# Causal mask of the row maxima moved from a matmul into VectorE's maximum, and query chunks made in every second step

## What is computed

```python
q = (x @ wq).reshape(b, s, H, QH).transpose(0, 2, 1, 3)      # b=2, s=1024, H=16, QH=192
q_pe = _rope(q_pe, cos, sin)
scores = jnp.einsum('bhqd,bhkd->bhqk', qs, ks_) * scale
causal = jnp.tril(jnp.ones((s, s), dtype=bool))
scores = jnp.where(causal, scores, jnp.finfo(scores.dtype).min)
attn = jax.nn.softmax(scores, axis=-1)
out = jnp.einsum('bhqk,bhkd->bhqd', attn, v)
```

## Time and profile before

| | |
|---|---|
| median of 3 runs | 1459.19 us (1459.08 to 1462.78) |
| profiled execution: its time, its span | 1459.05 us, 1457.2 us |
| PE busy (share of the span) | 1227.6 us (84%) |
| POOL busy | 961.9 us (66%) |
| DVE busy | 844.7 us (58%) |
| ACT busy | 626.2 us (43%) |
| mean granted clock of PE | 0.93 |

### The profile page before, as it was taken

How to read it: one execution, slowest core, us unless ns; L and a number is a source line. 1 busy time by engine, 2 the same in 40 slices (tenths; PEclk the granted TensorE clock), 3 DMA queues, 4 the chain that set the end, 5 groups by cost and what they waited for, 6 DMA issues and landing times. The chain is left out here.

```text
span 1457.2 us, 18876 instructions
## 1 busy us (share of the span) xinstructions
PE 1227.6 (84%) x5880; PEld 881.1 (60%) x5881; DVE 844.7 (58%) x1551; ACT 626.2 (43%) x1069; POOL 961.9 (66%) x700
## 2 busy tenths in 40 slices
PE   6974699999992489988998897689889998998797
PEld 5863455555551356666666666556666666666686
DVE  4578522222224667766676654767766776673567
ACT  3220233333320245565565564135655565565242
POOL 2025768888875457877788776557876787776454
PEclk9986799999995789999999998779999999999899
DMA  9348335555555000000000000000000000002001
GB/s 327 118 153 216 98 60 82 82 80 81 80 79 167 8 8 8 8 1 8 8 8 1 1 1 12 8 8 8 8 1 8 8 8 1 1 1 64 1 8 51
DMA packets 66509, 68.28 MB, mean 47 GB/s; under 512 B 15072, under 2 KB 59680, under 8 KB 66304
## 3 DMA queue, kind: packets, MB, share of 16 engines
q1 hardware_dynamic: 48336, 43.42, 10.0%
q0 software_dynamic: 15168, 20.72, 9.2%
q10 hardware_dynamic: 2928, 3.15, 0.7%
HBM read 46.17 MB, written 21.10 MB: 46 GB/s over the span
## 5 line engine op out<-in xcount | busy, mean ns | idle before, releaser
L1512 POOL TENSOR_TENSOR att_prob_lo<-att_prob,att_prob_hi 128x1024 fp32r<-128x1024 f32 (+1 forms) x160 | 346.7, 2167 | 114.1 <-ACT att_prob_hi L1448 114.0
L1555 DVE TENSOR_REDUCE att_peak<-all_bank 128x1 f32<-128x512 f32 (+3 forms) x384 | 207.4, 550 | 208.8 <-PE all_bank L1343 140.4
L1359 PE MATMUL all_bank<-att_q_hl,sequence_k_hl 128*128 128x512 f32 (+1 forms) x960 | 263.6, 385 | 0.0
L1382 PE MATMUL all_bank<-att_prob_hi,sequence_v_hl 128*128 128x512 f32 (+1 forms) x640 | 201.6, 396 | 35.3 <-POOL att_prob_lo L1512 19.1
L1441 ACT ACTIVATE att_prob<-all_bank 128x1024 f32<-128x1024 f32 (+1 forms) x160 | 150.6, 941 | 175.9 <-PE all_bank L1365 174.7
L1359 PEld LDWEIGHTS all_bank<-att_q_hl,sequence_k_hl 128*128 128x128 f32 x960 | 170.0, 192 | 26.1
L1340 PE MATMUL all_bank<-sequence_k_hl,att_q_hl 128*128 128x512 f32 (+3 forms) x384 | 171.0, 449 | 8.7 <-DVE att_peak L1555 8.3
L1448 ACT CAST att_prob_hi<-att_prob 128x1024 fp32r<-128x1024 f32 (+1 forms) x160 | 154.2, 964 | 5.1
L1327 PE MATMUL all_bank<-sequence_x_hl,sequence_w_hl 128*128 128x512 f32 x384 | 115.0, 438 | 46.3 <-DVE all_xT L1550 38.7
L1489 POOL TENSOR_TENSOR all_xT<-all_xT 128x512 f32<-128x512 f32 x64 | 82.4, 1288 | 106.1 <-DVE all_xT L1550 105.7
L916 PE MATMUL all_bank<-early_w_gu,moe_xgT 128*128 x316 | 148.9, 554 | 3.6 <-issue 2.4
(11 more groups left out here) (244 smaller groups left out, 2103.6 us busy)
## 6 DMA issues: line engine op xcount, KB each, us to landing
sequence_w_raw<-wqk_rows SPq DMA_DIRECT2D x16, 256.0 KB, 2.7
early_w_gu<-in_gate SPq DMA_DIRECT2D x16, 224.0 KB, 5.7
early_w_gu<-in_up SPq DMA_DIRECT2D x16, 224.0 KB, 5.8
early_w_down<-in_down SPq DMA_DIRECT2D x1, 3584.0 KB, 19.8
sums<-early_zero SPq DMA_DIRECT2D x18, 128.0 KB, 3.7
all_xT<-in_xT SPq DMA_DIRECT2D x4, 512.0 KB, 7.6
all_x_tok<-in_x SPq DMA_DIRECT2D x1, 2048.0 KB, 16.3
x_rows<-all_x_tok SPq DMA_DIRECT2D x4, 512.0 KB, 3.0
```

What stands on the lines that cost most here:

```text
L1359: nc.tensor.matmul(ps, k_hl[:, ks, j * P:(j + 1) * P], q_hl[n % 2][:, qs, :, i * BW + q0:(i + 1) * BW], start=g == 0, stop=False)
L1382: mm = nc.tensor.matmul(out, v_hl[:, vs, j, :], part[:, u % 3, half * WIDE:half * WIDE + 2 * w].rearrange("p (h m) -> p h m", h=2), start= ...
L1512: nc.gpsimd.tensor_tensor(prob_lo[:, u % 3, 0:w], prob[:, u % 2, 0:w], prob_hi[:, u % 3, 0:w].bitcast(F32), ALU.subtract).then_inc(lo_sb, 1)
L1555: nc.vector.tensor_reduce(peak[:, n % 2, part, t // 2, h, t % 2:t % 2 + 1], piece_ps[y % 2][:, 0:w], AX_X, ALU.max).then_inc(peak_sb, 1)
```

## The change

Two things change. In a diagonal piece the mask matmul is gone; DVE adds a table (`late_wide`, zeros and at its right end the causal triangle) to the piece and takes the maximum in the same instruction, writing the sum back to PSUM and the maximum to `peak`. For a row with two pieces the maximum of the first starts the second's, so that L1564 is gone. And the tables that place the work are new: query chunks in steps 0, 2, 4 and 6 instead of 0 to 3; eight of a pair's own pieces in its steps 0 to 3, the other 16 in steps 4 to 9 of the pair before (before: 3 own, 21 from step 2 of the pair before); weights, products and inversions moved to later steps.

```diff
-    NEXT_PIECES = [0, 0, 1, 2, 3, 3, 3, 3, 3, 3]
-    OWN_PIECES = [2, 1] + [0] * (NG - 2)
+    QUERY_AT = {0: 0, 2: 1, 4: 2, 6: 3}
+    NEXT_PIECES = [0, 0, 0, 0, 1, 3, 1, 3, 4, 4]
+    OWN_PIECES = [2, 3, 2, 1] + [0] * (NG - 4)
...
-    INVERT_AT = {1: (-1, 0), 2: (-1, 1), 3: (0, 0), 4: (0, 1), 5: (1, 0), 6: (1, 1), 7: (2, 0), 8: (2, 1)}
-    PRODUCT_AT = {3: -1, 5: 0, 7: 1, 9: 2}
+    INVERT_AT = {0: [(-1, 0)], 1: [(-1, 1)], 3: [(0, 0), (0, 1)], 5: [(1, 0)], 7: [(1, 1)], 8: [(2, 0)], 9: [(2, 1)]}
+    PRODUCT_AT = {0: -2, 2: -1, 4: 0, 8: 1}
...
                     mm = nc.tensor.matmul(ps[:, 0:w], q_hl[n % 2][:, 0, h, t * P:(t + 1) * P],
-                                          k_hl[:, 0, k0:k0 + w], start=True, stop=not diagonal)
-                    if diagonal:
-                        mm = nc.tensor.matmul(ps[:, w - P:w], bf["late_q"], bf["ident"], start=False, stop=True)
+                                          k_hl[:, 0, k0:k0 + w], start=True, stop=True)
...
-                    if x == 4 and n + 2 < PAIRS:
+                    if x == 7 and n + 2 < PAIRS:
                         weights_high(n + 2)
...
-                        if 1 <= x <= QC:
-                            q_low(n + 1, x - 1)
-                        if x < QC:
-                            rotate(n + 1, x)
+                        if x - 1 in QUERY_AT:
+                            q_low(n + 1, QUERY_AT[x - 1])
+                        if x in QUERY_AT:
+                            rotate(n + 1, QUERY_AT[x])
                     if u + AHEAD < STEPS:
                         low(u + AHEAD)
-                    if x == 5 and n + 2 < PAIRS:
+                    if x == 8 and n + 2 < PAIRS:
                         weights_low(n + 2)
...
                     dve.wait_ge(max_mm, n * NP + y + 1)
-                    nc.vector.tensor_reduce(peak[:, n % 2, part, t // 2, h, t % 2:t % 2 + 1], piece_ps[y % 2][:, 0:w],
-                                            AX_X, ALU.max).then_inc(peak_sb, 1)
+                    if diagonal:
+                        if part:
+                            dve.wait_ge(peak_sb, n * NP + y - 1)
+                        nc.vector.tensor_tensor_reduce(ps, ps, bf["late_wide"][:, WIDE - w:WIDE], 1.0, half if part else MASKED,
+                                                       ALU.add, ALU.max, whole).then_inc(peak_sb, 1)
+                    else:
+                        nc.vector.tensor_reduce(half, ps, AX_X, ALU.max).then_inc(peak_sb, 1)
...
-                    if i >= NB // 2:
-                        top = whole[:, n % 2, i]
-                        nc.vector.tensor_tensor(top, peak[:, n % 2, 0, i], peak[:, n % 2, 1, i], ALU.max).then_inc(whole_sb, 1)
-                        dve.wait_ge(whole_sb, n * (NB // 2) + i - NB // 2 + 1)
```

More of the change, by code:

```diff
@@ L63, in const_columns @@
     for name, width in (("ident", P), ("cos", QT * ROPE), ("sin", QT * ROPE), ("before", P), ("iota", P), ("headmask", P),
[L64 removed]
+                        ("late_q", P), ("late_k", P), ("late_cols", P), ("row", 1)):
         at[name] = (n, n + width)
@@ L96, in const_table @@
     put("late_k", np.where(f >= p, MASKED, 0.0))
-    q = np.arange(2 * P)[None, :] - P
-    put("late_cols", p == np.maximum(q + 1, 0))
+    put("late_cols", p == f + 1)
     put("row", p)
@@ L1253, in phase_attention @@
     block_needs = [1 + max(y for y in range(NP) if pieces[y][0] // 2 == i) for i in range(NB)]
-    NEXT_PIECES = [0, 0, 1, 2, 3, 3, 3, 3, 3, 3]
-    OWN_PIECES = [2, 1] + [0] * (NG - 2)
-    FIRST_PIECES = [3, 3, 2] + [0] * (NG - 3)
-    EARLY = NP - sum(FIRST_PIECES)
-    INVERT_AT = {1: (-1, 0), 2: (-1, 1), 3: (0, 0), 4: (0, 1), 5: (1, 0), 6: (1, 1), 7: (2, 0), 8: (2, 1)}
-    PRODUCT_AT = {3: -1, 5: 0, 7: 1, 9: 2}
+    QUERY_AT = {0: 0, 2: 1, 4: 2, 6: 3}
+    NEXT_PIECES = [0, 0, 0, 0, 1, 3, 1, 3, 4, 4]
+    OWN_PIECES = [2, 3, 2, 1] + [0] * (NG - 4)
+    EARLY = NP - sum(OWN_PIECES)
+    INVERT_AT = {0: [(-1, 0)], 1: [(-1, 1)], 3: [(0, 0), (0, 1)], 5: [(1, 0)], 7: [(1, 1)], 8: [(2, 0)], 9: [(2, 1)]}
+    PRODUCT_AT = {0: -2, 2: -1, 4: 0, 8: 1}
     def aside(n, x):
[L1264 to L1267, removed]
+        out = [("query", n + 1, QUERY_AT[x])] if n + 1 < PAIRS and x in QUERY_AT else []
+        out += [("piece", n, EARLY + sum(OWN_PIECES[:x]) + a) for a in range(OWN_PIECES[x])]
         if n + 1 < PAIRS:
@@ L1334, in piece @@
                     _, n, y = item
-                    t, h, _, k0, w, diagonal = pieces[y]
+                    t, h, _, k0, w, _ = pieces[y]
                     if n * NP + y >= 2:
@@ L1471, in _ @@
                     n, x, _, _ = at(u)
-                    made = n + 1 < PAIRS and x < QC
+                    made = n + 1 < PAIRS and x in QUERY_AT
                     if u + AHEAD < STEPS:
@@ L1476, in _ @@
                     if made:
-                        q_high(n + 1, x)
+                        q_high(n + 1, QUERY_AT[x])
                     if x in last_of:
                         sums(n, last_of.index(x))
-                    if x == 4 and n + 2 < PAIRS:
+                    if x == 7 and n + 2 < PAIRS:
                         weights_high(n + 2)
@@ L1536, in _ @@
                         product(n * NB + PRODUCT_AT[x])
+                product(PAIRS * NB - 2)
             @block.vector
@@ L1552, in peaks @@
                 def peaks(n, y):
-                    t, h, part, _, w, _ = pieces[y]
+                    t, h, part, _, w, diagonal = pieces[y]
+                    half, whole = (peak[:, n % 2, a, t // 2, h, t % 2:t % 2 + 1] for a in range(2))
+                    ps = piece_ps[y % 2][:, 0:w]
                     dve.wait_ge(max_mm, n * NP + y + 1)
-                    nc.vector.tensor_reduce(peak[:, n % 2, part, t // 2, h, t % 2:t % 2 + 1], piece_ps[y % 2][:, 0:w],
-                                            AX_X, ALU.max).then_inc(peak_sb, 1)
+                    if diagonal:
[5 more added lines that the diff above has]
+                        nc.vector.tensor_reduce(half, ps, AX_X, ALU.max).then_inc(peak_sb, 1)
                 def spread(n, i):
-                    top = peak[:, n % 2, 0, i]
+                    top = peak[:, n % 2, 1, i]
                     dve.wait_ge(peak_sb, n * NP + block_needs[i])
-                    if i >= NB // 2:
-                        top = whole[:, n % 2, i]
-                        nc.vector.tensor_tensor(top, peak[:, n % 2, 0, i], peak[:, n % 2, 1, i], ALU.max).then_inc(whole_sb, 1)
-                        dve.wait_ge(whole_sb, n * (NB // 2) + i - NB // 2 + 1)
                     if n:
@@ L1600, in _ @@
                         beside(item)
-                    if x in INVERT_AT:
-                        i, half = INVERT_AT[x]
+                    for i, half in INVERT_AT.get(x, ()):
                         if n * NB + i >= 0:
```

18 lines of the change are left out of this document (10 added, 8 removed).

## The result

The changed kernel took **1505.08 us** (median of 4 runs, 1503.77 to 1505.52) and the kernel before 1459.13 in the same rounds: ratio 1.0311, 95% interval 1.0289 to 1.0333. It is 3.1% slower; the forecast was 1523 in a range of 1462 to 1548. The profiled execution took 1505.52 us with a span of 1503.7.

The account below looks back on a forecast made before the run. PE was taken as the nearest bound, with query-to-sums chains behind two waits. Pairs at 47.85 us (+0.43, 14 times: 6.0) plus 1.6 for last pairs gave 1467; 56 of clock loss made 1523 us, range 1462 to 1548.

Parts of the forecast that it names:

- Pause A: PE's wait before V(1), the first value product of step 1: from 6.9 to 10.0 us after step 0 starts.
- Pause B: PE's wait before V(3), step 3's value product: work done at 18.4, product at 21.98, so 3.5 us.
- Step 0 to V(1): Stretch from a pair's start to step 1's first value product: same chain as before, 10.03 us.
- rival 3: Faster: the 1.26 us wait before V(3) is really POOL's, so a pair takes 44.2 us, 1414 in all; chance of faster 0.15.
- rival 1: The clock does not fall in the two pauses in steps 0 to 3: 1467 us; chance 0.10.
- the 0.53 us that V(6) was to wait: New PE wait after V(3), for block 2's sums: chain 8.5 us against 8.0 of PE work, 0.33 + 0.2.
- 25.34 and the wait: V(3) to the next step 0: 25.34 us of PE work, 24.92 before, plus 0.53 waiting for block 2's sums.
- I take 2.0 each: Clock loss behind each of the two pauses, between 1.5 and 2.7 us: 4.0 a pair, 56 us over 14 pairs.
- the forecast 0.8 for the eighth: Last pair of each sequence: five pieces more and two masks less, +0.8 us each, 1.6 in all.
- the 0.88 that was named as a sign: Sign in the changed trace: granted clock in a mid-phase pair below 1.00, about 0.88.
- The maxima were to cost 3.2 us more: DVE per pair: 16 second instructions at 0.2 us add 3.2, two dropped maxima of halves save 1.3.
- The accumulator's instruction: Second, 128x1 DVE instruction of each masked maximum: taken as 0.2 us, bounds 0.17 and 0.67.

Follow-up runs that it names:

- Experiment 3: Changed kernel with ACT's four copies of the sums placed ahead of its q_hl copy; 1421.83 us, ratio 0.9752.
- the filled kernel: Changed kernel with 6 and 12 useless 512-column matmuls a pair added on PE in steps 1 and 3; 1465.37 us, ratio 1.005.
- experiment 12: Kernel before with mask on DVE, ACT's copies of the sums first, and DVE doing the rope before the step's first maximum; 1375.43 us, ratio 0.9442.
- experiment 5: Changed kernel with query chunks back in steps 0 to 3, all else as changed; 1443.33 us, ratio 0.9905.
- experiment 6: Kernel before with ACT's four copies of the sums ahead of its q_hl copy; 1455.14 us (7 runs, 1436 to 1457).
- experiment 7: Kernel before with the mask on DVE and ACT's copies of the sums ahead of its q_hl copy; 1430.45 us.
- 8: Changed kernel with query chunks back in steps 0 to 3 and ACT's copies of the sums ahead of its q_hl copy; 1429.48 us.
- experiments 1: Kernel before with only the mask moved into DVE's maximum, all tables and work order as before; 1431.42 us, ratio 0.9814.
- experiment 10: Changed kernel with copies of the sums first and the spread split into four one-input DVE instructions; 1659.77 us, ratio 1.1391.

## Why the prediction came out as it did

- **The two pauses, and their length: right.** "Pause A: from 6.9 to 10.0" (3.1) measured 2.62; "Pause B: 3.5 us" measured 3.38. Step 0 to V(1) was forecast at 10.03 and took 9.97 (729.41 to 739.38).
- **Who ends them: right, and shown.** The row names POOL for V(3), yet ACT's last copy ended 0.14 us before it (752.30 + 0.36 = 752.66, against 752.80), while low(3) had ended at 743.80. The rows of POOL and ACT:

```profile
741.44 2.36 POOL L1508 TENSOR_TENSOR att_prob_lo<-att_prob,att_prob_hi 128x1024 fp32r<-128x1024 f32 x1 [0.75 <-ACT att_prob_hi L1444]
...
752.30 0.36 ACT L1456 COPY late_oT<-all_bank 64x256 f32<-64x256 f32 x1
```

  Experiment 3 moves only ACT's copies, and the wait is gone. This settles rival 3 (faster, since the wait is POOL's) against it.
- **The work without the clock: right, with some luck.** 47.85 us a pair were forecast, and the filled kernel with its clock at 1.00 has 47.90; 1465.4 in all stands beside the 1467 of rival 1. But the 0.53 us that V(6) was to wait is not there: at most 0.14 us lie between the piece before it (766.85 + 0.53) and V(6) at 767.52. (The terms written for that wait add up to 8.3, not 8.5.) The work of this stretch took longer instead, 26.03 us in the filled kernel where 25.34 and the wait had made 25.87.
- **The clock: the mechanism right, the term too large.** "I take 2.0 each", with its 4.0 a pair and 56 us, is the step that was mis-sized. Against the filled kernel V(1) to V(3) took 13.42 us in place of 11.88, and V(3) to the next step 0 27.59 in place of 26.03: 1.5 and 1.6, so 3.1 a pair and 43 us in 14. That is 13 of the 18 us between forecast and result. My lower bound of 1.5 was nearly the value for both; I had drawn the number upwards for a row whose low window was the longer one. Most of the rest lies in the stretches with the last pairs: at 3.56 us for the seventh pair and the forecast 0.8 for the eighth they should have grown by 4.4 us each, and they grew by 2.8 and 1.3. The granted clock of a pair was 0.93; the 0.88 that was named as a sign does not follow from the forecast's own 4.0 us. The Trainium skill (TensorE: Matmul & The Clock Gate, section HAM oscillation — how this bites in real kernels) says that waits between bursts leave the array cold for each burst; the windows of 0.60 and 0.64 agree.
- **DVE: the sum nearly right, by two errors that offset each other.** It is busy 35.7 us a pair (34.6 forecast, 32.7 before). The maxima were to cost 3.2 us more and cost 1.2 (13.05 before; 9.21 masked and 5.02 plain now). The accumulator's instruction is 0.142 us (0.2 forecast, bounds 0.17 to 0.67, so below the range, and above the 0.06 of the other estimate), and the rows show that the next masked pass starts at the same time as it:

```profile
749.06 0.75 DVE L1557 CUSTOM_DVE_ANT_0 all_bank<-all_bank,all_bf,att_peak 128x512 f32<-128x512 f32 x1
749.73 0.14 DVE L1557 DVE_READ_ACCUMULATOR2_ANT att_peak<- 128x1 f32 x1
749.73 0.76 DVE L1557 CUSTOM_DVE_ANT_0 all_bank<-all_bank,all_bf,att_peak 128x512 f32<-128x512 f32 x1
...
750.58 2.76 DVE L1568 SCALAR_TENSOR_TENSOR att_minus<-all_bf,att_peak 128x512 bf16<-128x512 bf16 x1
```

  The four spreads took 6.86 us a pair where they had taken 3.52, a term that the prediction left out: it costed one at 0.7 with room for twice that. At block 3 it took four times that (the last row), which cost nothing as long as the pause before V(3) was longer. Experiment 3 took that cover away and laid it bare.
- **What I did not see.** The prediction followed the chain and never asked why the rope comes behind a maximum. "Three times before a query, for the rope of the query before (2.0 us in all)" was in the first paragraph, and taken as given; turning that order was worth 55 us in experiment 12, more than the whole change.

## What to carry to other kernels

Follow a wait back through each engine's program order, not only through the data: here two in-order queues (ACT's q_hl copy ahead of its sums, DVE's maximum ahead of its rope) held more time than the work that was removed, and exchanging two neighbours in each was worth 83 us (experiment 3) and 55 us (experiment 12). What an exchange gives depends on the wait that comes next: that of experiment 3 gave 1 to 14 us in three other kernels. Work taken out of a stretch that waits for a chain only lengthens the wait, and in this kernel a wait of 2.6 or 3.4 us of TensorE cost another 1.5 or 1.6 us in clock. Waits of 6.2 us a pair in pieces of 1.2 and less cost none of it (experiment 5), those of 6.0 us in two pieces cost 3.1. After each removed wait look at which one is next before counting the gain: nine of the twelve main expectations missed, and five of these (3, 5, 6, 7 and 8) because the next wait took over.

## What the runs showed of the hardware

- **Useless work made it faster.** 18 matmuls a pair more and 40 us less: pauses of 2.62 and 3.38 us had cost 1.5 and 1.6 us of clock behind them. In the changed kernel's trace the 3.5 us behind each such pause show 0.51 to 0.70, in all 27 up to 1320 us.
- **Pauses of 2 us are at the edge.** Behind equal pauses the clock fell in some pairs and not in others of one execution (the 3.5 us behind the pause show 0.71 or less, or 1.00): behind 1.97 to 1.99 us in 4 of 14 (experiment 3), behind 1.98 and 1.99 in 5 of 12 (experiment 7), behind 2.06 to 2.09 in 9 of 12 (experiment 6), whose times scattered over 20 us. Behind pauses of 1.35 us and less (experiments 1 and 5) it stayed at 1.00.
- **DVE behind POOL.** The spread, a pass with two SBUF inputs, takes 0.69 us at least (changed kernel) and, in experiment 3, 2.80 beside a subtraction of 2.37 that started 0.12 us before it. A 128x128 TENSOR_SCALAR with one bf16 input takes 0.24 us at least and 2.47 at most. The Trainium skill (SBUF — State Buffer, section Who interferes with whom) says that a DVE instruction with two SBUF inputs contends with a GpSimd instruction that reads SBUF, that tensor_scalar can contend too, and that whoever issues first holds the shared ports for the whole instruction while the other is blocked. The rows agree: the spread ends 0.55 us behind the subtraction. That splitting such a pass can multiply the loss is what experiment 10 shows, 5.95 us for the four.
- **The masked maximum** costs 753 ns for 128x512 where it starts from the first piece's maximum and 702 where it does not, and 142 ns for reading its accumulator, of which a masked pass that follows directly sees nothing (749.73 above); the reduction alone takes 679 to 688.
